# A two-layer recurrent and mixture-of-experts kernel: first layer in another order, block transposes in another bank, products added in twos on GpSimd

## The chip, the cores and the metric

The kernel runs on one core of a Trainium2 chip. The metric is the device time of one execution in microseconds (us), lower is better. A run of the kernel here means one execution; the median of three is given, and beside it one execution that the hardware profiler recorded.

## What is computed

Tokens are 8 sequences of 256, 128 features each. There are two layers. Each adds to x the product of a selective scan (a Mamba block) and a gate that is the SiLU of a mixture of eight experts. In the first layer the mixture is a hard choice of one expert for each token; in the second all eight experts work on all tokens.

```python
x = L0_attn_x
xn = _layernorm(x, axis=-1)
s = _L0_attn_ref(xn, ...)          # scan with 16 states per feature
g = _silu(_L0_ffn_ref(xn, ...))    # each token goes to its best expert of 8
x = x + s * g
xn = _layernorm(x, axis=-1)
s = _L1_attn_ref(xn, ...)          # 256 inner features, 16 states, 4 heads
g = _silu(_L1_ffn_ref(xn, ...))    # all 8 experts, weighted
x = x + s * g

# inside the scan of the first layer
def step(h, inp):
    a, bx = inp
    h = a * h + bx
    return (h, h)
y = jnp.einsum('lbdn,bln->bld', hs, C_p)

# inside the experts of the first layer: LayerNorm again, then
h = jax.nn.relu(jnp.einsum('te,td,edf->tf', onehot, xn, W1) + b1[idx])
y = jnp.einsum('te,tf,efd->td', onehot, h, W2) + b2[idx]
y = y * gates
```

## The kernel before

The program is written by hand for each engine: every engine has its own instruction list, and semaphores tie the lists together. The 2048 tokens are handled in 4 pairs of sequences (512 tokens, `T`), and a tile is 128 partitions by 512 columns.

**Slots.** Every engine walks through the same numbered slots, 32 a pair, so the first layer has slots 0 to 127, and tables of numbers say what an engine issues in which slot. A slot has no time of its own: an engine does what its list says and waits only at semaphores. In slot s, `now(TABLE, s)` gives what is due. `CH0` is the table of the scan: state g (64 in all, 16 a pair) has slot 2g in pairs 0 to 2, and every one and a half slots in pair 3.

**One state of the scan.** ScalarE forms the decay (`decay0`, L1380), VectorE multiplies the drive (`drive0`, L799) and runs the scan over 512 columns (`scan0`, L807), GpSimd multiplies the states by C (`multiply0`, L1137), and TensorE adds the product into a PSUM bank by a product with the identity (`sum_product`, L1672, three slots behind, `SUM_LAG0`). There are four state tiles (`RING`) and three product tiles (`RING_Y`): VectorE may be four states ahead of GpSimd, GpSimd three products ahead of TensorE. The rows of B and C for a state come by DMA, broadcast to 128 partitions (`load_cb0`, L495, on SyncE's queue), six states ahead.

**The routed experts.** In slots 2 to 17 GpSimd scatters the 2048 normalised tokens by expert to DRAM (`scatter`, L1074, 16 indirect DMAs). The sorted tokens then make 15 blocks of 256, each of one expert. Block b has the slot 22 + 4b (`BLOCK_AT`):
- `load_block` (SyncE, L524) loads 256 tokens, three slots before; `load_pack` (GpSimd, L1081) gathers the expert's weights into one of two buffers, four slots before, and waits there until TensorE is done with block b - 2 (`blk_down`);
- `turn_block` (TensorE, L1555) transposes the tokens into `bank[OUT_BANK]`, columns 256 to 511; it waits until ScalarE has taken out the last block's result, which is in the same bank (`blk_out_ready`);
- `turn_in` (ScalarE, L1389) in the same slot copies it out, `up_block` (TensorE, L1567) one slot later, `relu` (ScalarE, L1397) two, `down_block` (TensorE, L1575 and the bias by L1576 with one row) three, `take_out` (ScalarE, L1403) four, `store_block` (SyncE, L529) six slots later.

**Other work of the first layer.** The heads of the next pair (`head0`, tables `PE0`, `ACT0`, `DVE0`, `POOL0`) form its projections, the convolution and the softplus; the tails (`tail`) finish a pair: y, LayerNorm, output product. `split_high`/`split_low` (L1256, L658) split eight gate matrices of the second layer into a high and a low part, loaded by `load_gate` (SyncE, L475). The first of these loads waits for `fold_conv` on GpSimd (L1145, L1147), which multiplies the convolution's taps into a weight and stands between slots 31 and 32 of GpSimd's list. From slot 86 GpSimd gathers each pair's expert outputs back (`fetch`, L1092), ScalarE takes the tanh (`tanh0`, L1410), VectorE gates (`gate0`, L850, and `gated0`, L857) and GpSimd adds x (L1169).

**The start.** Statistics and two LayerNorms of all four pairs (`first_stats`, `first_norm`, `second_stats`, `second_norm`): VectorE has the sums and applies mean and root (L676), GpSimd has the root (L1058). Then come the router's logits (TensorE, L1527), the choice and the slots of the tokens (`route_choice`, `route_slots`).

**The second layer**, from 330.6 us on, has loops of its own that the change doesn't touch, but for line numbers.

## Time and profile before

| | us |
|---|---|
| median of 3 runs | 807.91 |
| lowest and highest | 806.89, 808.41 |
| the profiled execution's own time | 802.77 |
| its span, first to last instruction | 800.9 |

The profiled execution is 5.1 us below the median; 1.9 us of it lie outside the span. Over the span TensorE (PE) is busy 80%, VectorE (DVE) 71%, GpSimd (POOL) 64%, ScalarE (ACT) 56%. These shares mix two layers with different limits. In the 40 slices of the page PE has 8 or 9 tenths in nearly every slice from the 18th on, the second layer, but between 0 and 9 in the slices before it. The chain that ended last covers only 21 us at the very end, so what holds the first layer has to be read from its waits and from the timeline of each engine.

### The profile page before, as it was taken

The page shows a single profiled execution, that of the slowest core. Times are in us where ns is not written, and L with a number is a line of the kernel's source. Part 1 is how long each engine was busy: PE and PEld are TensorE (multiplying, and loading weights), DVE is VectorE, ACT ScalarE, POOL GpSimd, SP SyncE. Part 2 cuts the span into 40 slices and gives each one's busy share as a digit, 9 for nine tenths or more (in the row PEclk, how much of TensorE's full clock was granted, in tenths as well). Part 3 has the DMA queues.
Part 4 walks back from the last instruction along what each step waited for, and adds up shares of the span by engine and source line. Part 5 has one row for each costly group of instructions (what it writes and reads, how often), then busy time and mean ns, then how long its engine had stood idle before and what let it go on. Part 6 is the DMA issues. An engine that isn't in the chain of part 4 may idle for free. (4 is left out here: it accounts for less than half of the span.)

```text
span 800.9 us, 8060 instructions
## 1 busy us (share of the span) xinstructions
PE 637.1 (80%) x1974; PEld 335.7 (42%) x1974; DVE 571.3 (71%) x921; ACT 450.4 (56%) x692; POOL 511.6 (64%) x419
## 2 busy tenths in 40 slices
PE   3545758989854587589998798998889998989995
PEld 2311446656631142344443454444445444444442
DVE  8688407646754984688676877775888775889983
ACT  2432425655463155885568584568665568675650
POOL 3268535424446763488786686786578786599983
PEclk9557779979985789799999999999999999999999
DMA  8277756798765871678476377677368576388860
GB/s 241 44 220 169 226 160 214 254 305 232 222 197 164 240 191 39 177 196 213 129 197 173 105 190 174 148 184 173 108 175 201 146 176 181 108 223 212 211 171 13
DMA packets 95791, 142.24 MB, mean 178 GB/s; under 512 B 8352, under 2 KB 37088, under 8 KB 95744
## 3 DMA queue, kind: packets, MB, share of 16 engines
q1 hardware_dynamic: 92560, 130.74, 61.6%
q0 software_dynamic: 3184, 10.98, 4.0%
q8 instruction: 16, 0.26, 0.1%
q14 instruction: 31, 0.25, 0.1%
HBM read 133.23 MB, written 8.45 MB: 177 GB/s over the span
## 5 line engine op out<-in xcount | busy, mean ns | idle before, releaser
L821 DVE TENSOR_TENSOR_SCAN state<-decay,bank 128x512 f32<-128x512 f32 x128 | 155.8, 1217 | 8.6 <-issue 0.9
L1742 PE MATMUL bank<-xw,wu 128*128 128x512 f32 x256 | 138.2, 622 | 27.9 <-DVE hid L935 27.4
L1123 POOL TENSOR_TENSOR product<-state,CB 128x512 f32<-128x512 f32 x96 | 122.9, 1281 | 53.1 <-DVE state L821 50.7
L935 DVE TENSOR_TENSOR hid<-sg,bank 128x512 f32<-128x512 f32 x128 | 85.9, 671 | 67.6 <-PE bank L1742 64.2
L1752 PE MATMUL bank<-hid,wd 128*128 128x512 f32 x256 | 133.3, 603 | 0.0
L1435 ACT ACTIVATE sg<-bank 128x512 f32<-128x512 f32 x128 | 75.2, 597 | 101.9 <-PE bank L1653 92.2
L1125 POOL TENSOR_TENSOR product<-product 128x512 f32<-128x512 f32 x96 | 124.3, 1294 | 7.5
L1672 PE MATMUL bank<-product,early 128*128 128x512 f32 x128 | 81.2, 734 | 50.9 <-POOL product L1137 50.9
L814 DVE TENSOR_TENSOR bank<-bank,CB 128x512 f32<-128x512 f32 x128 | 88.7, 693 | 12.8 <-DMA CB<-crow 11.5
L1742 PEld LDWEIGHTS bank<-xw,wu 128*128 128x128 f32 x256 | 43.7, 191 | 109.3 <-issue 60.5
L1137 POOL TENSOR_TENSOR product<-state,CB 128x512 f32<-128x512 f32 x44 | 56.0, 1280 | 50.4 <-DVE state L807 50.0
L1372 ACT ACTIVATE decay<-delta,negA 128x510 f32<-128x510 f32 x128 | 82.1, 709 | 2.6 <-DVE delta L787 2.2
L807 DVE TENSOR_TENSOR_SCAN state<-decay,bank 128x512 f32<-128x512 f32 x64 | 77.9, 1217 | 7.3 <-ACT decay L1380 3.8
L1651 PE MATMUL bank<-XH,wh 128*128 128x512 f32 x128 | 75.1, 587 | 8.4 <-ACT sg L1435 7.4
L1752 PEld LDWEIGHTS bank<-hid,wd 128*128 128x128 f32 x256 | 48.6, 193 | 37.3 <-issue 30.5
L1119 POOL TENSOR_TENSOR product<-state,CB 128x512 f32<-128x512 f32 x32 | 40.8, 1276 | 34.7 <-PE bank L1664 18.1
L1672 PEld LDWEIGHTS bank<-product,early 128*128 128x128 f32 x128 | 25.2, 225 | 78.4 <-POOL product L1137 54.7
L1653 PE MATMUL bank<-XH,wl 128*128 128x512 f32 x128 | 52.7, 412 | 0.0
L1081 POOL DMA_INDIRECT wd<-pack_dram,rows_of x15 | 14.8, 986 | 59.4 <-PE bank L1576 58.9
L1652 PE MATMUL bank<-XL,wh 128*128 128x512 f32 x128 | 52.6, 411 | 0.0
L1182 POOL TENSOR_TENSOR xw<-XR,cwb 128x512 f32<-128x512 f32 x32 | 42.1, 1316 | 9.9 <-DMA cwb<-cwrow 4.4
L1380 ACT ACTIVATE decay<-delta,negA 128x510 f32<-128x510 f32 x64 | 43.7, 709 | 2.2 <-DVE delta L787 2.2
(200 smaller groups left out, 1039.0 us busy)
## 6 DMA issues: line engine op xcount, KB each, us to landing
CB<-crow SPq DMA_DIRECT2D x256, 256.0 KB, 5.0
CB<-crow SPq DMA_DIRECT2D x44, 512.0 KB, 5.9
cwb<-cwrow SPq DMA_DIRECT2D x32, 256.0 KB, 5.6
szm<-crow SPq DMA_DIRECT2D x11, 512.0 KB, 5.3
cwb<-crow SPq DMA_DIRECT2D x9, 512.0 KB, 6.3
xw<-Wg_dram SPq DMA_DIRECT2D x8, 256.0 KB, 6.6
wu<-Wu_dram SPq DMA_DIRECT2D x8, 256.0 KB, 7.1
wd<-Wd_dram SPq DMA_DIRECT2D x8, 256.0 KB, 6.8
```

The lines of the kernel that those rows point to most:

```text
L807: v.tensor_tensor_scan(state[:, g % RING, :], place0(g), drive, 0.0, ALU.mult, ALU.add).then_inc(state_ready.sem, 1)
L814: v.tensor_tensor(drive, dx, CB[:, c % ROWS, 1, :], ALU.mult).then_inc(drive_ready.sem, 1)
L821: v.tensor_tensor_scan(state[:, c % RING, :], decay[:, PLACE[c], :], drive, 0.0, ALU.mult, ALU.add).then_inc(state_ready.sem, 1)
L935: v.tensor_tensor(hid[:, u % 2, :], sg[:, PLACE[u], :], bank[UP_BANK][:, :], ALU.mult).then_inc(hid_ready.sem, 1)
L1123: p.tensor_tensor(addend, state[:, c % RING, :], cs, ALU.mult).then_inc(state_used.sem, 1)
L1125: ins = p.tensor_tensor(product[:, e % PRODS, :], product[:, e % PRODS, :], addend, ALU.add)
L1372: a.activation(by_batch(decay[:, PLACE[c], :])[:, :, 1:], by_batch(delta[:, m, :])[:, :, 1:], ACT.Exp, scale=negA[:, c:c + 1]).then_inc(de ...
L1435: a.activation(sg[:, PLACE[u], :], bank[stream_bank(u)][:, :], ACT.Silu).then_inc(silu_ready.sem, 1)
L1651: t.matmul(dst, wh[:, e, ws], XH[:, :], start=True, stop=False)
L1672: t.matmul(bank[Y_BANK][:, :], ident[:, :], product[:, g % RING_Y, :], start=(c == 0), stop=(c == N - 1)).then_inc(summed.sem, 1)
L1742: t.matmul(bank[UP_BANK][:, :], wu[:, e, 128 * f:128 * f + 128], xw[:, e % 2, :], start=True, stop=True).then_inc(up_ps.sem, 1)
L1752: ins = t.matmul(bank[OUT_BANK][:, :], wd[:, u, :], hid[:, u % 2, :], start=(u == 0), stop=(u == UNITS - 1))
```

## The change

- **Order.** The single `BLOCK_AT` becomes tables by step. With `UP_AT` = 22 + 4b, the transpose is two slots before, its copy one before, relu one after, the down product three after, the result is taken out four after: no two steps of a block that hand over to each other stand in the same slot. Pack loads stand six slots before, block loads five before. The scatters start at slot 0. The heads' slots move forward, the splits are 8 slots apart instead of 6 with three slots between high and low, and tanh and gates have later slots.
- **Banks.** The block's transpose goes to `bank[HID_BANK]`, columns 0 to 255, where the up product writes afterwards; it waits for the first two relus of the block before, no longer for its result to be taken out.
- **Packs.** Three weight buffers (`PACKS`) instead of two. The columns of x move to other tiles for it.
- **Fold first.** `fold_conv` stands before GpSimd's slots.
- **Products in twos.** `GROUP` = 2: GpSimd adds two products (32 more additions of 128x512), and TensorE adds 32 sums instead of 64, through two product tiles and an addend; `sum_group` stands four slots behind the second.
- **Start.** The LayerNorms are applied by ScalarE (`shifted`, 32 activations of 128x128); VectorE forms only the negated mean times the root (8 small operations of 128x4). One of the four logits products stands before, one behind the dt and row products, and the wait for `late_in` behind all of them.
- **Small.** The bias row of the down product becomes a full 128-row product with a matrix whose first row is one (`top_row`). ScalarE's decays run four states ahead instead of two. A wait of the expert weights' loads on a pair's y falls away, and these loads start four slots later.

```diff
-RING_Y = 3
+GROUP = 2
-PE0 = {3: "xin", 12: "z", 16: "dt", 18: "row"}
-ACT0 = {4: "xin", 11: "th", 17: "dt", 19: "row", 23: "ln"}
-DVE0 = {6: "tap1", 7: "tap2", 8: "tap3", 12: "xs", 14: "zx", 20: "rest", 26: "delta"}
-POOL0 = {21: "less"}
+PE0 = {1: "xin", 9: "z", 13: "dt", 15: "row"}
+ACT0 = {2: "xin", 8: "th", 14: "dt", 16: "row", 19: "ln"}
+DVE0 = {4: "tap1", 5: "tap2", 6: "tap3", 9: "xs", 11: "zx", 17: "rest", 21: "delta"}
+POOL0 = {18: "less"}
...
-SUM_LAG0, SUM_LAG1 = 3, 4
+SUM_LAG0, SUM_LAG1 = 4, 4
...
-SCATTER_AT = [2 + k for k in range(NT)]
-BLOCK_AT = [22 + 4 * b for b in range(BLOCKS)]
-SPLIT_AT = [34 + 6 * e for e in range(E)]
-GATHER_AT = [86, 91, 96, 111]
-TANH_AT = [89, 94, 99, 114]
-GATE_AT = [90, 95, 109, 116]
+SCATTER_AT = list(range(NT))
+UP_AT = [22 + 4 * b for b in range(BLOCKS)]
+TURN_AT, TURN_IN_AT = [at - 2 for at in UP_AT], [at - 1 for at in UP_AT]
+RELU_AT, DOWN_AT, TAKE_AT = ([at + lag for at in UP_AT] for lag in (1, 3, 4))
+PACK_AT, LOAD_AT, STORE_AT = ([at + lag for at in UP_AT] for lag in (-6, -5, 6))
+PACKS = 3
+SPLIT_AT = [30 + 8 * e for e in range(E)]
+SPLIT_LOW_AT = [at + 3 for at in SPLIT_AT]
+GATHER_AT = [86, 91, 95, 112]
+TANH_AT = [91, 95, 99, 116]
+GATE_AT = [92, 96, 109, 118]
+AHEAD = 4
...
@@ first_norm, second_norm of VectorE
-                normalise(x_rows[:, q, :, :], x_rows[:, q, :, :], mv1[:, q, :, :], rstd1[:, q, :], xn_ready)
+                negated_mean(shift1, mv1, rstd1, rstd1_ready, q, shift1_ready)
...
@@ load_pack of GpSimd
-                if b >= 2:
-                    pool.wait_ge(blk_down.sem, blk_down.at0(0, b - 1))
+                if b >= PACKS:
+                    pool.wait_ge(blk_down.sem, blk_down.at0(0, b - PACKS + 1))
...
@@ multiply0 of GpSimd
-                if g >= RING_Y:
-                    pool.wait_ge(summed.sem, summed.at0(0, g - RING_Y + 1))
-                p.tensor_tensor(product[:, g % RING_Y, :], state[:, g % RING, :], cb_pair(g)[:, 0, :], ALU.mult).then_inc(state_used.sem, 1)
+                q = g // GROUP
+                cs = cb_pair(g)[:, 0, :]
+                if g % GROUP == 0:
+                    if q >= PRODS:
+                        pool.wait_ge(summed.sem, summed.at0(0, q - PRODS + 1))
+                    p.tensor_tensor(product[:, q % PRODS, :], state[:, g % RING, :], cs, ALU.mult).then_inc(state_used.sem, 1)
+                else:
+                    pool.wait_ge(group_ready.sem, group_ready.at0(0, q))
+                    p.tensor_tensor(addend, state[:, g % RING, :], cs, ALU.mult).then_inc(state_used.sem, 1)
+                    pool.wait_ge(state_used.sem, state_used.at0(0, g + 1))
+                    ins = p.tensor_tensor(product[:, q % PRODS, :], product[:, q % PRODS, :], addend, ALU.add)
...
@@ GpSimd, after the roots
+            fold_conv()
             head0("less", 0)
-            for s in range(UNITS):
-                slot0(s)
-            fold_conv()
-            for s in range(UNITS, PAIRS * UNITS):
+            for s in range(PAIRS * UNITS):
                 slot0(s)
...
@@ turn_block of TensorE
+                if b == 0:
+                    pe.wait_ge(xnT_read.sem, xnT_read.at0(0, PAIRS))
                 if b >= 1:
-                    pe.wait_ge(blk_out_ready.sem, blk_out_ready.at0(0, b))
-                if b == 0:
-                    pe.wait_ge(lg0_ready.sem, lg0_ready.at0(0, 1))
+                    pe.wait_ge(blk_relu.sem, blk_relu.at0(0, FT * (b - 1) + 2))
                 for k in range(2):
-                    last = t.transpose(bank[OUT_BANK][:, BLOCK + 128 * k:BLOCK + 128 * k + 128], blk_x[:, b % 2, k, :], ident[:, :])
+                    last = t.transpose(bank[HID_BANK][:, 128 * k:128 * k + 128], blk_x[:, b % 2, k, :], ident[:, :])
...
@@ down_block of TensorE
-                    last = t.matmul(dst, ones128[0:1, :], pack[0:1, b % 2, PACK_COLS - D:PACK_COLS], start=False, stop=True)
+                    last = t.matmul(dst, top_row[:, :], pack[:, b % PACKS, PACK_COLS - D:PACK_COLS], start=False, stop=True)
```

How it moves instructions. TensorE's queue, one block in the middle of the blocks, before: the names are `hid` (tokens of a block, to be transposed), `product` (a state's product, to be added), `sg` (the transposed tokens, then the relu's result), `wd` (the pack of weights).

```order
L1555 MATMUL bank<-early,hid 128x128 x2
L1672 MATMUL bank<-product,early 128x512
L1567 MATMUL bank<-sg,wd 128x256 x4
L1672 MATMUL bank<-product,early 128x512
L1575 MATMUL bank<-wd,sg 128x128 x4
L1576 MATMUL bank<-wd,ones 128x128
L1575 MATMUL bank<-wd,sg 128x128 x4
L1576 MATMUL bank<-wd,ones 128x128
```

The same place now:

```order
L1721 MATMUL bank<-product,early 128x512
L1611 MATMUL bank<-sg,wd 128x256 x4
L1601 MATMUL bank<-early,hid 128x128 x2
L1623 MATMUL bank<-wd,sg 128x128 x4
L1624 MATMUL bank<-wd,top_row 128x128
L1623 MATMUL bank<-wd,sg 128x128 x4
L1624 MATMUL bank<-wd,top_row 128x128
```

The transpose of the next block has moved from behind the down product to between the up and the down product of this block, and one of the two sums is gone.

GpSimd's queue while it scatters (`wu` holds the normalised tokens, `CB` the rows of C), before:

```order
L1137 TENSOR_TENSOR product<-state,CB 128x512
L1074 DMA sorted_in<-wu,slot_of 3840x128 x2
L1137 TENSOR_TENSOR product<-state,CB 128x512
L1074 DMA sorted_in<-wu,slot_of 3840x128 x2
L1137 TENSOR_TENSOR product<-state,CB 128x512
```

and now:

```order
L1154 TENSOR_TENSOR product<-state,CB 128x512
L1087 DMA sorted_in<-wu,slot_of 3840x128 x2
L1158 TENSOR_TENSOR product<-state,CB 128x512
L1160 TENSOR_TENSOR product<-product 128x512
L1087 DMA sorted_in<-wu,slot_of 3840x128 x2
```

An addition stands in the queue for every four scatters; the first scatter stands ahead of the first product.

## Rows read from the trace of the kernel before

**Rows 1.** Windows by stage: PE, PEld, DVE, ACT, POOL busy; PEclk, DMA share, GB/s.

```profile
43.50:85.80 42.30, 21.33 (x29) 6.31 (x29) 31.74 (x35) 10.64 (x17) 35.13 (x32) 0.66 0.71 187
85.80:232.00 146.20, 124.24 (x564) 85.22 (x564) 84.36 (x120) 79.34 (x155) 59.85 (x52) 0.92 0.73 225
232.00:330.60 98.60, 50.09 (x118) 20.84 (x118) 60.82 (x115) 44.64 (x74) 52.24 (x46) 0.76 0.64 176
330.60:800.90 470.30, 423.55 (x1204) 211.71 (x1204) 362.27 (x494) 299.84 (x422) 353.80 (x277) 0.98 0.64 164
```

**Rows 2.** Waits, 85.8 to 232 us: who for whom, total us, times, longest.

```profile
POOL wd L1081 <- PE bank L1576: 58.9, 13, 11.2
...
PE bank L1555 <- DMA hid<-sorted_in: 11.4, 2, 8.5
```

**Rows 3.** Waits of SyncE's DMA queue, 0 to 330 us, same columns.

```profile
SPq L475 <- POOL later L1147: 18.1, 1, 18.1
```

**Rows 4.** Timeline of GpSimd: start, us, instruction; the convolution's fold.

```profile
105.82 2.08 POOL L1145 TENSOR_TENSOR w_cv<-w_cv,later 128x256 f32<-128x256 f32 x3
```

**Rows 5.** Timeline of TensorE, one undisturbed block; counts are passes, two a product.

```profile
156.09 0.38 PE L1555 MATMUL bank<-early,hid 128*128 128x128 f32 x2
156.30 1.02 PE L1672 MATMUL bank<-product,early 128*128 128x512 f32 x2
157.16 1.95 PE L1567 MATMUL bank<-sg,wd 128*128 128x256 f32 x8
158.95 1.02 PE L1672 MATMUL bank<-product,early 128*128 128x512 f32 x2
160.05 1.16 PE L1575 MATMUL bank<-wd,sg 128*128 128x128 f32 x8
161.13 0.48 PE L1576 MATMUL bank<-wd,ones 1*128 1x128 f32 x2
...
163.68 0.41 PE L1555 MATMUL bank<-early,hid 128*128 128x128 f32 x2 [0.56 <-ACT hid L1403]
```

**Rows 6.** Timeline of ScalarE: the four relus of that block.

```profile
158.35 1.64 ACT L1397 ACTIVATE sg<-bank,wd 128x256 f32<-128x256 f32 x4 [0.19 <-PE bank L1567]
```

**Rows 7.** Timeline of GpSimd while it scatters.

```profile
59.77 0.95 POOL L1074 DMA_INDIRECT sorted_in<-wu,slot_of  x1 [0.30 <-issue]
...
63.49 0.96 POOL L1074 DMA_INDIRECT sorted_in<-wu,slot_of  x1 [0.30 <-issue]
...
77.17 1.01 POOL L1074 DMA_INDIRECT sorted_in<-wu,slot_of  x1 [0.17 <-issue]
```

**Rows 8.** The page's costliest groups: the second layer's additions on GpSimd.

```profile
L1125 POOL TENSOR_TENSOR product<-product 128x512 f32<-128x512 f32 x96 | 124.3, 1294 | 7.5
```

**Rows 9.** Timeline of TensorE: the first block's transpose.

```profile
85.77 0.69 PE L1555 MATMUL bank<-early,hid 128*128 128x128 f32 x2 [2.88 <-DMA hid<-sorted_in]
```

**Rows 10.** Timelines of SyncE, GpSimd, ScalarE and VectorE: last block's store to second gate.

```profile
231.83 0.47 SPq L529 DMA_DIRECT2D sorted_out<-hid  x1
...
238.13 1.00 POOL L1092 DMA_INDIRECT sg<-sorted_out,slot_of  x1 [6.47 <-DMA sorted_out<-hid]
...
244.45 1.27 ACT L1410 ACTIVATE yfT<-sg,hp 128x128 f32<-128x128 f32 x4 [9.23 <-DMA sg<-sorted_out,slot_of]
...
258.52 1.34 DVE L850 SCALAR_TENSOR_TENSOR yfT<-yfT,sg 128x512 f32<-128x512 f32 x1 [4.53 <-ACT yfT L1410]
```

**Rows 11.** Timeline of VectorE: last scan of the first layer, first step of the second.

```profile
310.68 1.22 DVE L807 TENSOR_TENSOR_SCAN state<-decay,bank 128x512 f32<-128x512 f32 x1
...
330.63 0.69 DVE L793 TENSOR_TENSOR bank<-delta,xs 128x512 f32<-128x512 f32 x1
```

**Rows 12.** Timeline of VectorE: the router's logits.

```profile
34.61 0.29 DVE L702 TENSOR_TENSOR sz<-bank,brb 128x128 f32<-128x128 f32 x1 [6.85 <-PE bank L1527]
```

**Rows 13.** One line's durations in ns, min/median/max: the convolution's taps on VectorE.

```profile
L748 DVE SCALAR_TENSOR_TENSOR sp_e<-xpad,early,sp_e x12: 726/745/1793, 14.7 to 207.5; 128x512 f32<-128x512 f32 x12
```

**Rows 14.** Timeline of TensorE: a down product after a wait.

```profile
170.27 1.98 PE L1575 MATMUL bank<-wd,sg 128*128 128x128 f32 x8 [2.67 <-ACT sg L1397]
```

156 lines of the change are left out of this document (94 added, 62 removed).

## The prediction, made before the changed kernel had run

> **What bounds the kernel now.** I read the windows by stage first [rows 1]. The second layer, from 330.6 us on, has TensorE (PE) busy 423.6 of 470.3 us at a granted clock of 0.98, and no line of it is changed: it stays at 470.3 us. The first layer takes 330.6 us, and in none of its stages is one engine full, but for the 146.2 us of the expert blocks, where PE is busy 124 us. So the question is what the engines wait for there. The waits of that stage [rows 2] name GpSimd's pack loads first: 58.9 us in 13 times, each for the end of a down product of PE. GpSimd's queue is in order, so behind that wait stand the products, behind them VectorE's scans (four state tiles) and PE's own sums. Next is PE's wait for a block of tokens, 11.4 us in two pieces. SyncE's own waits say where it comes from [rows 3]: it stood 18.1 us at the first gate matrix's load, which waits for the convolution's fold on GpSimd, and the next block's load is queued behind. The fold ran at 105.8 us [rows 4], because GpSimd itself sat in a pack load's wait.
>
> PE's timeline shows the floor below these stalls: an undisturbed block goes from transpose to transpose in 163.68 - 156.09 = 7.59 us [rows 5]. The stage took, from the first transpose at 85.77 [rows 9] to the last store at 231.83 [rows 10], 146.1 us for 15 blocks, 9.74 each.
>
> **Start: earlier, but it doesn't reach the end.** VectorE waited 6.85 us for the logits, to 34.61 [rows 12]; the LayerNorms leave its queue and the heads' products move ahead of the last logits. The slot loop began at 43.5 (where the first window of [rows 1] begins) and can come at most those 6.85 us sooner, and at worst no sooner; since the choice and the slots of the tokens hang on these logits and nothing else is late, I take 4.8, to 38.7. But then GpSimd sets the pace until the scatters are out. Two slots cost it 63.49 - 59.77 = 3.72 us (two scatters, one product) [rows 7]. Now four slots also hold an addition, 1.29 us [rows 8] and 0.06 of issue: 2 x 3.72 + 1.35 = 8.8 us. The first scatter goes at about 37.7, slot 3 ends at about 49.4, twelve more slots take 3 x 8.8 = 26.4, so the last scatter ends at about 76.2 instead of 77.17 + 1.01 = 78.2 [rows 7]. The chain from there to the first transpose was 85.77 - 78.18 = 7.6 us and stays: **-1.9 us** (-4.0 and +2.9 at the ends of the start's range). The moved slots of the heads are hidden here: PE is busy half of that stage, ScalarE a quarter [rows 1].
>
> **Block stage: -27 us.** A third pack buffer puts GpSimd's wait at the down product of block b - 3, nine slots behind the up product for which the pack comes, and the load stands six before it: three slots of slack where there was one. Fold first removes SyncE's 18.1 us. So PE's own cycle is left. Its parts by starts [rows 5]: sum 0.86; up product 1.79; down product (160.05 to 163.12, less the wait) 3.0; transpose 0.25. One sum goes. The transpose doesn't wait 0.56 for the result's removal any more. The bias product of one row takes 0.42 (161.13 to 161.55), a full one 0.27 (an eighth of 1.16 for a pass, two passes): -0.15 twice. That leaves 0.86 + 1.79 + 2.7 and a gap: relus end 1.64 after their start, which came 158.35 - 157.16 = 1.19 after the up product's [rows 6], so down starts 2.9 after up, and in between stand 1.79 of up and the next block's transpose. Sum: 0.86 + 2.9 + 2.7 = 6.5 us. In this gap the four heads of a pair are hidden; the tails (y, yn, s) partly.
>
> Other engines in four slots: busy time of the stage over its 15 blocks [rows 1] is 84.4 / 15 = 5.6 us on VectorE, 79.3 / 15 = 5.3 on ScalarE and 59.9 / 15 + 1.35 = 5.3 on GpSimd. All are below PE, but VectorE has more than its mean in the first half of a pair, where heads and tails stand and its tail and PE's wait for each other in turn, and ScalarE's logarithm with its table loads once let PE wait 2.67 us [rows 14]. DMA moved 225 GB/s at a share of 0.73 [rows 1]: the same bytes in 117 us want a share of 0.9, so landings will be late at times. Between 6.5 and the old 9.7 I take 7.7, near the undisturbed 7.59, since what goes (1.7 us) is in part eaten by the first half of the pair and by DMA. 15 x 7.7 = 115.5, and 2 for the low clock of the first block and 1.5 from last down to store: 119 against 146.1.
>
> A rule of the Trainium skill speaks on one term: "TensorE: Matmul & The Clock Gate", section "Why this matters for your kernels", says that a product with 32 rows takes as long as one with 128. By it the full bias row would give nothing, and the block 0.3 us more, 4.5 us over the stage. The trace shows the one-row product at 0.42 against 0.27, and the measurement goes first.
>
> **Gathers: -1.5 us.** The second gate came 258.52 - 231.83 = 26.7 us after the last store [rows 10]. In the new order: the store lands after 238.13 - 231.83 = 6.3, and GpSimd has three products and two additions of 1.3 ahead of the second fetch, 6.5. The gathers are 4 x (0.95 + 0.30), as the scatters cost [rows 7]; the tanh began 244.45 - 238.13 - 4.8 = 1.5 behind them and takes 1.3 [rows 10]: store + 6.3 + 4.8 + 6.5 + 4.8 + 1.5 + 1.3 = 25.2. A store that lands sooner, since the expert weights load later now, would give up to 3 more. GpSimd is full here, where before it waited for VectorE.
>
> **Pair 3 and the end: -2 us.** From the second gate to the end of the last scan VectorE needed 311.9 - 258.5 = 53.4 us, to the second layer's first step 18.7 more, a chain of heads through PE, ScalarE and VectorE [rows 11]. GpSimd now has 16 products, 8 additions, four gathers, three small roots and residuals in it: 31.6 + 4.8 + 5 = 41, below 53. So VectorE still leads. The last gate now stands behind the softmax of the next layer's head instead of ahead of it; so its wait for the last gathers leaves the chain. No row prices that; between 0 and -4 I take 2.
>
> **Sum.** -1.9 - 27 - 1.5 - 2 = -32.4: the span 800.9 becomes 768.5. The profiled execution lay 5.1 us below the median of 807.91; I take the difference from the median: **775.5 us**.
>
> **The rivals.**
> - *PE's cycle is reached.* The engines interlock without loss and a block takes 7.0: 105 + 3.5 = 108.5 in the stage, 10.5 us less; with 3 more in the gathers 762. For it: the heads fit into the gap. Against: VectorE's load in the first halves and DMA at a share near 1.
> - *DMA is next.* Packs and blocks land late and a block takes 8.5: 131 us, -15 instead of -27, 787.5. For it: the undisturbed block above ran while DMA had 0.89, and the whole stage already had 0.73 [rows 1]. Against: packs are asked for six slots ahead, some 11 us.
> - *The additions are on the path.* GpSimd gets 32 x 1.35 = 43 us. Eight lie among the scatters and are counted; if the eleven from slot 84 on all show (15 us), less the 2.6 counted in the gathers, it is 788. For it: GpSimd has the gathers there. Against: 52 of 98.6 us busy [rows 1].
> - *Two inputs, one port.* The Trainium skill ("SBUF — State Buffer", section "Who interferes with whom") says that a VectorE operation with two inputs in SBUF and a GpSimd operation that reads SBUF exclude each other. The taps show something like it: 745 ns in the middle, 1793 at most [rows 13]. Scan and drive read one of their inputs from PSUM. Some 10 operations a pair could each wait up to 1.05, 40 us if all did; the taps' median says that few do, and I count 3 us, within the forecast's range.
> - *Slower: PE falls to the low clock.* Granted clock in the block stage was 0.92. After a wait of 2.67 us the same eight passes took 1.98 instead of 1.16 us [rows 5, 14]. With one sum less PE has a gap of 0.9 us in every block. If the clock fell to 1.2 GHz for the whole stage, PE's 5.4 us would be 9.3 and the block about 11: 165 + 3.5 against 146.1, +22.4 instead of -27, 825. It decides from some 65% of the blocks at the low clock; below that the change still wins. Against: at 156 to 164 us PE kept 0.6 us idle a block at the full clock.
> - *The change does not do what it says:* if turn, up and relu still wait in turn, a block takes 7.6 to 8.5, which lies in the cases above, as GpSimd's and SyncE's long waits go in any case.
>
> **How the numbers follow.** Forecast 0.60 (766 to 784), PE's cycle reached 0.14, DMA 0.11, additions 0.10, low clock 0.04, anything near no change 0.01. A measurement of this kernel can tell about 0.2% from no change, 1.6 us. Faster: 0.95; same: 0.01; slower: 0.04. The range holds the forecast and reaches to the first three rivals: 757 to 792.
>
> **What would show it.** In the profile after: the first transpose at about 84 us; the last block's store near 203; GpSimd's waits at the pack loads near nothing, SyncE's at the first gate matrix gone; transposes 7 to 8 us apart; the second layer's first step near 298 and 470 us behind it. If transposes are 8.5 apart with PE waiting for DMA, the second rival holds; if VectorE waits for GpSimd after slot 84, the third; a clock well below 0.9 in the block stage, the slow one. I am wrong if the second layer's 470 us change or if the scatter stage gives back more than the start gains.

## The result, and the profile after

The changed kernel takes **784.9 us** (median of 4 runs, 779.8 to 786.0) where the kernel before takes 808.2 beside it: a ratio of **0.969**, 95% interval 0.964 to 0.975. It is faster by 23 us where the prediction had 32. The profiled execution took 784.66 us (span 782.8); that of before 802.77, which was 5 us under its own median, so between the two traces there are 18.1 us to be found. Three executions further below, one each of e6, e7 and e8, took over 1.5% longer than the fastest of their kernel; the ratios leave them out, the medians don't, and that of e6 is the one of its trace.

The windows by stage of the changed kernel, cut at its first block transpose, its last store, its second gate and the first step of the second layer (columns as in [rows 1]: busy time of PE, PEld, DVE, ACT, POOL; then granted clock, DMA share, GB/s):

```profile
42.50:82.40 39.90, 13.37 (x14) 3.92 (x14) 25.06 (x27) 12.57 (x18) 35.63 (x32) 0.89 0.65 165
82.40:208.45 126.05, 102.93 (x530) 80.14 (x530) 84.61 (x120) 72.84 (x149) 82.74 (x67) 0.89 0.84 259
208.45:237.92 29.47, 5.28 (x6) 1.30 (x6) 17.60 (x20) 9.58 (x20) 21.69 (x19) 0.59 0.70 200
237.92:309.56 71.64, 41.06 (x94) 16.46 (x94) 50.11 (x99) 35.94 (x56) 47.66 (x41) 0.67 0.62 172
309.56:782.80 473.24, 426.29 (x1204) 212.83 (x1204) 362.96 (x494) 300.02 (x422) 353.82 (x277) 0.97 0.65 163
```

Read against [rows 1] and [rows 9 to 11], the block stage gained by far the most, 146.1 to 126.0 us. The start gained 3.4 (first transpose at 82.4 instead of 85.8). The way from the last store to the second gate got longer, 26.7 to 29.5; from there to the end of the last scan shorter, 53.4 to 49.3; from there to the second layer longer, 18.7 to 22.3; and the second layer, whose code is the same, took 473.2 instead of 470.3. The sum is -3.4 - 20.0 + 2.8 - 4.1 + 3.6 + 3.0 = -18.1.

The waits of the block stage (who waited for whom, total us, times, longest):

```profile
POOL wd L1094 <- PE bank L1624: 11.2, 6, 4.2
...
PE bank L1601 <- DMA hid<-sorted_in: 13.2, 3, 4.7
...
PE bank L1556 <- DVE wu L684: 7.5, 2, 3.7
...
DVE wu L684 <- POOL rstd_t L1071: 5.8, 2, 2.9
```

GpSimd's 58.9 us of waits for pack buffers [rows 2] are 11.2, and SyncE's 18.1 us at the first gate matrix [rows 3] are gone. TensorE's waits for tokens are not: 13.2 us in three pieces, of which 4.7 are the first block's. In the kernel before they were 11.4 in two pieces, and one of them, 2.9 us, was the first block's too ([rows 2], [rows 9]). Behind the first block TensorE waited 8.5 us before and waits 8.5 us now: once for block 2 then, twice for 4.1 and 4.4 us now. One late block is cured, and two others are late now.

An undisturbed block, on TensorE's timeline (start, us, instruction; a product of 32-bit floats is two passes):

```profile
100.32 0.41 PE L1601 MATMUL bank<-early,hid 128*128 128x128 f32 x2 [0.16 <-ACT sg L1435]
101.09 1.16 PE L1623 MATMUL bank<-wd,sg 128*128 128x128 f32 x8 [0.36 <-ACT sg L1435]
102.09 0.39 PE L1624 MATMUL bank<-wd,top_row 128*128 128x128 f32 x2
102.31 1.06 PE L1623 MATMUL bank<-wd,sg 128*128 128x128 f32 x8
...
103.43 1.02 PE L1721 MATMUL bank<-product,early 128*128 128x512 f32 x2
104.29 1.89 PE L1611 MATMUL bank<-sg,wd 128*128 128x256 f32 x8
106.40 0.41 PE L1601 MATMUL bank<-early,hid 128*128 128x128 f32 x2 [0.22 <-ACT sg L1435]
```

It takes 6.08 us from transpose to transpose where it took 7.59 [rows 5]. The stage took 8.4 a block all the same, some 30 us in all above such blocks. Two kinds of place account for a good half of this (18 us, by e7 below). First, tokens that come late; second, the root of the LayerNorm on GpSimd. Both stand in the timelines of SyncE, PE, GpSimd and VectorE:

```profile
82.66 1.78 SPq L533 DMA_DIRECT2D hid<-sorted_in  x1
...
92.36 0.69 PE L1601 MATMUL bank<-early,hid 128*128 128x128 f32 x2 [4.08 <-DMA hid<-sorted_in]
92.85 1.92 PE L1623 MATMUL bank<-wd,sg 128*128 128x128 f32 x8
...
118.65 1.27 POOL L1158 TENSOR_TENSOR product<-state,CB 128x512 f32<-128x512 f32 x1 [2.87 <-DVE state L818]
120.00 1.26 POOL L1160 TENSOR_TENSOR product<-product 128x512 f32<-128x512 f32 x1
121.22 1.04 POOL L1071 TENSOR_TENSOR rstd_t<-veps_t,half 128x4 f32<-128x4 f32 x1
...
122.30 1.36 DVE L684 TENSOR_SCALAR wu<-bank,mv_t,rstd_t 128x128 f32<-128x128 f32 x4 [2.90 <-POOL rstd_t L1071]
...
123.72 1.12 PE L1556 MATMUL bank<-early,wu 128*128 128x128 f32 x4 [3.73 <-DVE wu L684]
```

Block 1's tokens were asked for at 82.66 and let TensorE start at 92.36; the eight passes behind that wait took 1.92 us instead of 1.06, at the lower of the two clocks (granted clock 0.50 from 92.3 to 94.8 us). At 118 to 124 us the small root waits in GpSimd's queue behind a product and its addition, VectorE waits 2.90 us for the root and TensorE 3.73 us for VectorE. The same happens one pair later. The addition is the change's own: in the kernel before, the root stood behind a product alone, and VectorE waited for it once, 1.8 us.

From the last store to the second gate (SyncE, GpSimd, ScalarE, VectorE), to be read beside [rows 10]:

```profile
208.45 0.47 SPq L538 DMA_DIRECT2D sorted_out<-hid  x1
...
216.11 1.00 POOL L1105 DMA_INDIRECT sg<-sorted_out,slot_of  x1 [5.52 <-DMA sorted_out<-hid]
...
227.88 0.99 POOL L1105 DMA_INDIRECT sg<-sorted_out,slot_of  x1
...
236.61 1.28 ACT L1448 ACTIVATE yfT<-sg,hp 128x128 f32<-128x128 f32 x4 [11.72 <-DMA sg<-sorted_out,slot_of]
...
237.92 0.82 DVE L861 SCALAR_TENSOR_TENSOR yfT<-yfT,sg 128x512 f32<-128x512 f32 x1 [4.86 <-ACT yfT L1448]
```

The store took 7.7 us to land instead of 6.3; the second fetch came 11.8 us behind the first, as counted (11.3); but ScalarE began 8.7 us behind the start of the second fetch, where 4.8 + 1.5 = 6.3 had been counted.

The last head (ScalarE, PE, VectorE), to be read beside [rows 11]:

```profile
286.62 1.28 ACT L1314 ACT_TABLE_LOAD   x1
...
291.17 1.10 PE L1561 MATMUL bank<-xs,later 128*96 128x512 f32 x2 [3.38 <-ACT sz L1369]
292.95 2.08 PE L1677 MATMUL bank<-XNP,later 128*128 128x512 f32 x2 [0.68 <-ACT rows L1377]
...
296.66 2.07 PE L1561 MATMUL bank<-rows,w_dt 32*128 32x512 f32 x2
```

The head's exponential needs a table load of 1.28 us here. In the kernel before, the scans' last decays, exponentials too, stood close ahead of this head and had brought the table off the chain; now the last decays are done sooner, another function has been loaded since, and the load lies in the chain. TensorE's wait for the same product grows from 1.10 to 3.38 us, and behind it two products take 2.08 and 2.07 us instead of 1.12 and a sum 1.91 instead of 1.02, at a granted clock of 0.58 from 291.0 to 298.7 us. The load and the slower products make 4.1 us; since this head also began 0.6 us sooner against the last scan's end, 3.6 are lost. This is read from the traces; no run tried another order on ScalarE. The Trainium skill ("ScalarE: Activation LUTs", section "What ACT_TABLE_LOAD costs") gives 1283 ns for a load and 2.66 us with a drain for a switch. The trace agrees on the load; it shows the next activation 1.29 us behind the load's start and the load right behind the activation ahead of it, so no drain beside it.

### The profile page after: what moved, and what is told of

The parts are those of the page before. It is cut to its first block and busy times, and to the rows that moved or that the text cites. A ratio compares the mean times of both kernels' runs of the same rounds, so it can differ in the third digit from the quotient of the medians.

```text
span 782.8 us, 7991 instructions
## 1 busy us (share of the span) xinstructions
PE 609.7 (78%) x1910; PEld 328.3 (42%) x1910; DVE 567.7 (73%) x899; ACT 461.5 (59%) x724; POOL 555.9 (71%) x451
## 5 line engine op out<-in xcount | busy, mean ns | idle before, releaser
L1792 PE MATMUL bank<-xw,wu 128*128 128x512 f32 x256 | 140.0, 629 | 28.1 <-DVE hid L946 27.8
L1136 POOL TENSOR_TENSOR product<-state,CB 128x512 f32<-128x512 f32 x96 | 122.9, 1280 | 54.7 <-DVE state L832 52.2
L1473 ACT ACTIVATE sg<-bank 128x512 f32<-128x512 f32 x128 | 75.3, 597 | 102.7 <-PE bank L1701 91.2
L946 DVE TENSOR_TENSOR hid<-sg,bank 128x512 f32<-128x512 f32 x128 | 85.9, 671 | 67.7 <-PE bank L1792 64.2
L1138 POOL TENSOR_TENSOR product<-product 128x512 f32<-128x512 f32 x96 | 124.2, 1294 | 7.5
L1721 PE MATMUL bank<-product,early 128*128 128x512 f32 x64 | 46.9, 824 | 59.7 <-POOL product L1160 59.7
L1699 PE MATMUL bank<-XH,wh 128*128 128x512 f32 x128 | 75.7, 591 | 8.4 <-ACT sg L1473 7.4
L1132 POOL TENSOR_TENSOR product<-state,CB 128x512 f32<-128x512 f32 x32 | 40.8, 1276 | 37.2 <-DVE state L832 19.6
L1721 PEld LDWEIGHTS bank<-product,early 128*128 128x128 f32 x64 | 13.1, 251 | 76.7 <-POOL product L1160 58.3
L1160 POOL TENSOR_TENSOR product<-product 128x512 f32<-128x512 f32 x32 | 41.5, 1298 | 2.5
L1410 ACT ACT_TABLE_LOAD x32 | 41.1, 1283 | 0.6
```

Of the source, the lines that this page charges most:

```text
L946: v.tensor_tensor(hid[:, u % 2, :], sg[:, PLACE[u], :], bank[UP_BANK][:, :], ALU.mult).then_inc(hid_ready.sem, 1)
L1136: p.tensor_tensor(addend, state[:, c % RING, :], cs, ALU.mult).then_inc(state_used.sem, 1)
L1138: ins = p.tensor_tensor(product[:, e % PRODS, :], product[:, e % PRODS, :], addend, ALU.add)
L1410: a.activation(by_batch(decay[:, PLACE[c], :])[:, :, 1:], by_batch(delta[:, m, :])[:, :, 1:], ACT.Exp, scale=negA[:, c:c + 1]).then_inc(de ...
L1473: a.activation(sg[:, PLACE[u], :], bank[stream_bank(u)][:, :], ACT.Silu).then_inc(silu_ready.sem, 1)
L1699: t.matmul(dst, wh[:, e, ws], XH[:, :], start=True, stop=False)
```

## The experiments

All runs are compared with the kernel before on the same chip, by ratio and 95% interval; the stages are read from each run's trace, at the same five cuts as above. The table has the numbers on which the verdicts rest (us). The runs come in four groups, in which the kernel before took 808.2 (changed), 810.6 (again, e1 to e3), 805.4 (e4 to e6, v1) and 809.3 us (v1 again, e7, v2, e8): medians compare within such a group, ratios across them. Each row has one trace, so a stage's time is that of one execution.

| kernel | median | ratio (95%) | first transpose | blocks | store to gate | to last scan | to layer 2 | layer 2 |
|---|---|---|---|---|---|---|---|---|
| before | 808.2 | 1 | 85.8 | 146.1 | 26.7 | 53.4 | 18.7 | 470.3 |
| changed | 784.9 | 0.969 (0.964-0.975) | 82.4 | 126.0 | 29.5 | 49.3 | 22.3 | 473.2 |
| changed, again | 785.2 | 0.969 (0.964-0.974) | 82.9 | 126.5 | 28.9 | 49.5 | 21.0 | 476.3 |
| e1 tokens 8 ahead | 779.6 | 0.963 (0.958-0.968) | 81.8 | 119.0 | 28.7 | 50.5 | 23.9 | 474.6 |
| e2 root sooner | 777.8 | 0.961 (0.956-0.966) | 82.3 | 118.1 | 28.1 | 51.7 | 22.5 | 473.9 |
| e3 no additions | 775.7 | 0.958 (0.953-0.963) | 78.2 | 122.4 | 27.4 | 49.3 | 22.0 | 473.8 |
| e4 before + fold first | 797.6 | 0.990 (0.983-0.997) | 86.8 | 136.6 | 26.8 | 53.4 | 18.7 | 470.2 |
| e5 before + third pack | 800.3 | 0.990 (0.982-0.997) | 86.2 | 139.8 | 26.8 | 53.4 | 21.1 | 472.3 |
| e6 before + both | 792.1 | 0.979 (0.971-0.987) | 85.9 | 135.6 | 26.6 | 53.6 | 18.7 | 477.3 |
| v1 = e1 + e2 + e3 | 766.3 | 0.948 (0.942-0.955) | 75.9 | 114.5 | 28.1 | 50.3 | 21.2 | 475.2 |
| v1 again | 764.7 | 0.944 (0.941-0.948) | 76.0 | 116.4 | 28.7 | 49.6 | 21.6 | 473.6 |
| e7 = e1 + e2 | 766.6 | 0.949 (0.945-0.954) | 81.9 | 107.8 | 28.7 | 51.8 | 21.2 | 467.3 |
| v2 added in blocks only | 762.5 | 0.940 (0.935-0.944) | 75.3 | 113.1 | 25.8 | 49.4 | 21.8 | 477.7 |
| e8 = v1 + one-row bias | 769.4 | 0.950 (0.946-0.955) | 76.3 | 118.5 | 27.9 | 49.2 | 22.0 | 473.1 |

The theory: the change gained by the order and the waits it took away, and lost some 9 us of that to late tokens and to a root behind an addition. The main rival: the additions themselves are too dear, wherever they stand.

**The changed kernel again**, no edit.

> The changed kernel once more, unaltered, as the measure for the runs beside it. Expected 785 us (780 to 788), a ratio to the kernel before of 0.970 (0.964 to 0.975). It also asks which waits of the first trace are the program's and which are chance. The waits of the block stage that the order fixes (3.7 us twice for yn, the late token blocks 1 and 8 at about 4 us each, the 17 us of VectorE for wh) should come again within 1 us; the dip of the granted clock to 0.76 at 375 to 380 us in the second layer, which the kernel before didn't have behind the same 1.3 us wait, should be gone if it was chance, and the second layer then takes 470 us again instead of 473.2.

The time came again. The waits for yn came within 1 us. VectorE's for `wh` did not (13.2 us instead of 17.6), nor did the tokens': behind the first block TensorE waited 13.4 us in four times instead of 8.5 in two, and block 1's transpose came at 95.8 instead of 92.4. So a late block is the program's, how late is chance. The second layer did not go back to 470 (476.3).

**e1: tokens eight slots ahead.**

```diff
-PACK_AT, LOAD_AT, STORE_AT = ([at + lag for at in UP_AT] for lag in (-6, -5, 6))
+PACK_AT, LOAD_AT, STORE_AT = ([at + lag for at in UP_AT] for lag in (-6, -8, 6))
```

> One edit of the changed kernel: the block of tokens is asked for eight slots ahead of its up product instead of five. Theory (late blocks): TensorE's two waits for a block, 4.1 and 4.4 us, with the passes at 1.2 GHz behind them (about 1.5 and 2), go or shrink below 1 us; the first layer loses 6 to 10 us, ratio 0.958 to 0.963. Rival (the transfers themselves are the limit, share 0.84 in the stage): the earlier block only pushes pack loads back, TensorE waits for packs or other blocks instead, and the time stays within 2 us (0.967 to 0.972). Rival 3: the load now stands ahead of a store or of the gate matrices in SyncE's queue and waits for its buffer to come free, so that the stage gets longer by some us.

The theory holds: -5.6 us, and 7.0 to 7.5 in the block stage, some of it given back behind it. TensorE's timeline at blocks 1 and 2:

```profile
87.97 0.42 PE L1601 MATMUL bank<-early,hid 128*128 128x128 f32 x2 [0.16 <-DMA hid<-sorted_in]
97.00 0.44 PE L1601 MATMUL bank<-early,hid 128*128 128x128 f32 x2 [0.76 <-DMA hid<-sorted_in]
```

Block 1 starts 4.4 us sooner than in the changed kernel. The transfers were late because they were asked for late. Behind the first block TensorE waits for tokens more than 1 us only once, 1.9 us.

**e2: the root one slot sooner.**

```diff
-POOL_TAIL = {39: "yn2"}
+POOL_TAIL = {38: "yn2"}
```

> One edit of the changed kernel: GpSimd's small root of yn stands one slot earlier in its queue, ahead of the product and the addition of the slot (2.6 us) that it stood behind. Theory (root behind the addition): VectorE's waits for the root, 2.90 us each at 122.3 and 187.3, fall below 1, TensorE's two waits of 3.7 us for yn fall to about 1, and the low clock at 124 to 128 goes; 4 to 7 us off the stage, ratio 0.961 to 0.966. Rival (VectorE was late itself, and the root only came last): the root now waits for VectorE's sums instead, GpSimd's product and addition behind it come later, and the time stays within 1.5 us.

The theory holds: -7.4 us, at the better end of the expected ratio, and 7.9 to 8.4 in the block stage, a little more than expected. VectorE and PE, at the place that is shown above for the changed kernel:

```profile
121.32 1.36 DVE L684 TENSOR_SCALAR wu<-bank,mv_t,rstd_t 128x128 f32<-128x128 f32 x4
...
122.73 0.66 PE L1556 MATMUL bank<-early,wu 128*128 128x128 f32 x4 [0.74 <-DVE wu L684]
```

VectorE doesn't wait, TensorE waits 0.74 us instead of 3.73 and keeps its clock (four transposes in 0.66 us instead of 1.12).

**e3: no additions.** Each product goes to TensorE as it is, 64 sums instead of 32, through three product tiles; a sum stands three slots behind its product instead of four. The main lines:

```diff
-                    ins = p.tensor_tensor(product[:, q % PRODS, :], product[:, q % PRODS, :], addend, ALU.add)
...
+                if g >= 3:
+                    pool.wait_ge(summed.sem, summed.at0(0, g - 3 + 1))
+                p.tensor_tensor(product[:, g % 3, :], state[:, g % RING, :], cb_pair(g)[:, 0, :], ALU.mult).then_inc(state_used.sem, 1)
```

> The changed kernel without the additions: each state product goes to TensorE as it is, 64 sums more for TensorE in the first layer and none of GpSimd's 32 additions. Its order, third pack buffer, fold and bias product stay. Theory (the additions give TensorE a sum a block and cost GpSimd 1.3 us for it; the two nearly cancel): the scatter stage is shorter by 5 x 1.35 = 4 to 7 us, the block 0.9 us of TensorE longer (a cycle of about 6.9 instead of 6.1) but with no wait for the root, the gathers 2.6 us shorter: together within 5 us either way, ratio 0.964 to 0.974. If the additions carry the gain of the block stage, 15 x 0.9 = 13 us go and the ratio is 0.984. If they stand on the path behind slot 84, as one rival of the prediction has it, it is 8 to 12 us faster, 0.956.

It is 9.5 us faster than the changed kernel. That is the price of the last case, but not its place. Against the changed kernel run beside it, 4.7 us lie ahead of the first transpose, 4.1 in the block stage and 1.5 at the gathers. GpSimd's scatters, four slots apart:

```profile
48.64 1.03 POOL L1087 DMA_INDIRECT sorted_in<-wu,slot_of  x1 [0.30 <-issue]
...
56.30 0.96 POOL L1087 DMA_INDIRECT sorted_in<-wu,slot_of  x1 [0.30 <-issue]
```

Four slots take 7.66 us, and 9.07 in the changed kernel. In the block stage undisturbed transposes are 5.9 to 7.2 us apart instead of 6.0 to 6.4: there an addition does spare TensorE something, and the kernel with additions loses it again at its waits, the two for the root among them.

**e4, e5, e6: parts of the change in the kernel before.** e4 puts the fold ahead of head "less" and of the first slot; e5 makes three pack buffers, for which the columns of x move to other tiles; e6 does both.

```diff
+            fold_conv()
             head0("less", 0)
-            for s in range(UNITS):
-                slot0(s)
-            fold_conv()
-            for s in range(UNITS, PAIRS * UNITS):
+            for s in range(PAIRS * UNITS):
                 slot0(s)
```

The third buffer (main lines):

```diff
-                if b >= 2:
-                    pool.wait_ge(blk_down.sem, blk_down.at0(0, b - 1))
-                p.indirect_dma_start(pack[:, b % 2, :], None, w["pack"], bass.IndirectOffsetOnAxis(rows_of[:, b:b + 1], 0)).then_inc(pack_in[b % 2].sem, 16)
+                if b >= 3:
+                    pool.wait_ge(blk_down.sem, blk_down.at0(0, b - 2))
+                p.indirect_dma_start(pack[:, b % 3, :], None, w["pack"], bass.IndirectOffsetOnAxis(rows_of[:, b:b + 1], 0)).then_inc(pack_in[b % 3].sem, 16)
```

> The kernel before with one edit: the convolution's fold stands first in GpSimd's and ScalarE's order, ahead of the scatters' slots, as in the changed kernel. Theory: SyncE's 18.1 us at the first gate matrix's load goes, block 2's tokens come in time, and TensorE loses most of its 11.4 us of waits for tokens; but GpSimd's 58.9 us of waits for pack buffers stay, and a part of what TensorE gains turns into waits for packs: block stage -4 to -8 of 146, ratio 0.990 to 0.995. Rival (pack buffers alone hold the stage): the same time within 0.3%. Rival 2 (the fold's matrix work delays the scatters by its 1 to 2 us): slower by 0.2%.

> The kernel before with one edit: three pack buffers in place of two; order, sums and bias product stay. Theory: GpSimd's 58.9 us of waits for down products fall below 15; the fold and with it SyncE's gate matrix come sooner by themselves, as GpSimd was late with the fold for a pack's sake; block stage -10 to -14 of 146, ratio 0.982 to 0.988. Rival (GpSimd's waits were slack, and TensorE's order of sum, transpose, up, relu, down sets 9.7 us a block): -3 us or less, ratio above 0.996.

> The kernel before with both edits, fold first and three pack buffers: all that the change does to waits for buffers and loads, and nothing of its order, additions and bias product. Theory: the block comes down to the undisturbed 7.6 us of the kernel before plus late transfers, a stage of about 128 (-18 of 146), ratio 0.978 (0.972 to 0.984). The changed order is then worth the 8 to 10 us from there to the changed kernel without its additions (ratio 0.958 in the run before). Rival (the order carries the gain): -8 us or less here, ratio above 0.989.

e4 and e5 are each 1% faster than the kernel before, with intervals from 0.3 to 1.8%. The waits of the block stage of e4:

```profile
POOL wd L1081 <- PE bank L1574: 52.1, 13, 9.5
```

and of e5:

```profile
POOL product L1138 <- DVE state L808: 72.8, 23, 11.3
...
POOL wd L1082 <- PE bank L1577: 2.2, 2, 1.6
```

e4 left 52 of the 58.9 us of GpSimd's waits where they were and still took 9.4 us off the stage, more than the 4 to 8 expected; e5 took away all but 2.2 of them and gained 6.3, about half of what was expected. GpSimd then waited 72.8 us for VectorE's states instead, where it had waited 26.7: the largest wait of the profile was mostly slack. In the traces both edits together gave 10.5 us of the stage, not the 15.7 of their sum. A reason is at hand: each also cures part of what the other does, since SyncE's 18.1 us at the gate matrix are 9.8 in e5 already. The expected 18 was too much by 7.5: where nothing was late, the old order's transposes stayed 7.6 to 9.0 us apart. The whole times don't show the overlap, though. e4 and e5 have 0.990 each, and e6 has 0.979, which is what the two make together and what was expected (0.978). With intervals of 0.8% to either side this decides nothing, and how far the two gains overlap stays open.

So by the traces about 10.5 of the 20 us of the block stage belong to fold and buffers. The step from there to the kernel without additions (135.6 to 122.4, 13.1 us) is everything else: the new order and banks, the full bias product (2 to 4 us by e8), the moved heads and splits, the decays further ahead. The additions as placed took 3.6 back. Order alone was not run, so its share is a difference and not a measurement.

**v1: the three gains together.**

> The changed kernel without the additions, with the block of tokens asked for eight slots ahead and GpSimd's root of yn one slot sooner: the three edits that each gained, together. Theory (they remove different waits): without the additions TensorE still waited 9.3 us for tokens; 6 of them go. The root then waited for no addition, so it gives 1 to 2 at most. Expected 769 us (765 to 773), ratio 0.951 (0.945 to 0.956). Rival (their gains are the same microseconds, since a freer GpSimd already let the loads come sooner): 774 to 776, ratio 0.957 as without the additions alone.

It came at the fast end of what was expected: 766.3 us, 0.948, and 764.7, 0.944, in a second set of runs, whose expectation was

> The version without additions, with the two earlier placements, once more, as the measure for the three runs beside it: a ratio of 0.948 (0.943 to 0.953), a block stage of 114.5 us with pure blocks at 5.9 to 6.0.

**e7: both placements, additions kept.** The two diffs of e1 and e2.

> The changed kernel with its additions kept and the two earlier placements (tokens eight slots ahead, root of yn one slot sooner). The two placements alone gave 7.1 and 8.2 us in the block stage of the changed kernel, 126. Theory (they remove different waits, and the additions then cost what they cost in the first scatters and the gathers, but give TensorE a sum a block): T0 stays at 82, block stage 112 (110 to 116), total 771 (768 to 775), ratio 0.953 (0.949 to 0.958), 4 to 5 us above the version without additions. Rival (the additions cost nothing once the placements are mended): ratio 0.948, as without them. Rival 2 (GpSimd is full in the block stage): 118 there, ratio 0.960.

The windows of its block stage and its second layer:

```profile
81.89:189.66 107.77, 94.59 (x530) 71.66 (x530) 88.94 (x121) 73.32 (x149) 83.75 (x68) 0.97 0.94 309
...
291.31:758.60 467.29, 422.27 (x1204) 210.85 (x1204) 362.38 (x494) 299.90 (x422) 353.67 (x277) 0.98 0.67 165
```

The block stage was expected at 112 us and took 107.8, the shortest of all, with the DMA engines at a share of 0.94 and 309 GB/s: the transfers had not been the limit at 0.84. v1's stage is 6.7 to 8.6 longer, and its first transpose 5.9 sooner. The medians are 1.9 us apart, and the intervals overlap. In total e7 is at 0.949, which is the first rival's number and not the theory's 0.953. So once tokens and root are in time the additions cost 1.9 us, within the noise of nothing, where they cost the changed kernel 9.5: that was mostly the price of their place, and the rival (they are too dear wherever they stand) has no support. By the traces they gain in the block stage what they cost in the scatters, but the size of that gain is uncertain, for e7's trace is its fastest execution (760.4 us, its median 766.6) and v1's second one its slowest (767.8, median 764.7).

**v2: additions only in the block stage.** Products of slots 16 to 79 are added in twos, the others go one by one; the placements are those of v1. The main lines:

```diff
+TWOS = range(4, 20)
+SUMS0 = [u for q in range(PAIRS * N // 2) for u in ([(2 * q, 2 * q + 1)] if q in TWOS else [(2 * q,), (2 * q + 1,)])]
...
+                for n, gs in enumerate(SUMS0):
+                    if s == CH0[gs[-1]] + (4 if len(gs) == 2 else 3):
+                        sum_mixed(n)
```

> The version without additions and with the two earlier placements, but with the 16 additions of the groups from slot 16 to 79 put back: products are added in twos only where the expert blocks run, and go to TensorE one by one in the scatter and gather stages. Theory (an addition buys TensorE time only where TensorE is full, which is the block stage: 104.8 of 114.5 us busy there): the first block's transpose stays at 76, the block stage gets 0.86 a block shorter where nothing else holds it, 114.5 becomes 106 to 110, and the rest stays: 760 us (757 to 764), ratio 0.941. Rival (DMA, at a share of 0.88 in that stage, or VectorE is next at once): 113 to 115 in the stage, ratio 0.947. Rival 2 (GpSimd's longer queue delays the scans there): slower, 0.951.

```profile
75.30:188.38 113.08, 97.70 (x533) 73.71 (x534) 90.14 (x122) 76.73 (x155) 83.38 (x67) 0.95 0.90 297
...
285.35:763.00 477.65, 431.63 (x1204) 214.84 (x1204) 362.71 (x494) 300.17 (x422) 353.81 (x277) 0.96 0.66 162
```

762.5 us is the best median, 6% below the kernel before and 3% below the changed one. It doesn't prove its reason. The stage took 113.1 us in the trace, not 106 to 110. Late tokens are not why: behind the first block TensorE waited 3.3 us for them, and 2.4 in v1's second trace. The last block shows another reason (ScalarE, GpSimd, SyncE):

```profile
183.24 0.38 ACT L1443 ACTIVATE hid<-bank 128x256 f32<-128x256 f32 x1 [0.91 <-PE bank L1626]
...
184.23 1.27 POOL L1160 TENSOR_TENSOR product<-state,cwb 128x512 f32<-128x512 f32 x1 [5.56 <-PE bank L1725]
...
188.38 0.47 SPq L545 DMA_DIRECT2D sorted_out<-hid  x1
```

The first single product behind the pairs, slot 80, goes to the tile of the last pair (`TILE0`), so GpSimd waits 5.56 us for TensorE's sum of that pair. SyncE's loads of the rows of B and C wait for GpSimd (4.6 us), and the last store stands behind them: it goes 4.8 us after its result was taken out, in e7 1.1 us after. These 3.6 us are the edit's own, at the place where pairs end; without them the stage would be 109.5 us, an estimate from the two traces that no run tried. A part is given back behind the store (25.8 us to the gate, v1 28.1 and 28.7). And the intervals of v1 (0.941 to 0.948) and v2 (0.935 to 0.944) overlap. That the two placements and this one together beat the changed kernel is certain; that v2 beats v1 is not.

**e8: the one-row bias product in v1.**

```diff
-                    last = t.matmul(dst, top_row[:, :], pack[:, b % PACKS, PACK_COLS - D:PACK_COLS], start=False, stop=True)
+                    last = t.matmul(dst, ones128[0:1, :], pack[0:1, b % PACKS, PACK_COLS - D:PACK_COLS], start=False, stop=True)
```

> The version without additions and with the two earlier placements, with the bias product of one row put back in place of the full one of 128 rows (two per block, 30 in all). It was sized in the prediction at 0.15 us a product, 4.5 us over the stage; the changed kernel's trace shows starts 0.22 apart where it was 0.42. Theory: down products take 0.4 us longer a block; where TensorE is full (9 or 10 of 15 blocks) this shows, pure blocks at 6.3 instead of 5.9, stage +4 to +6, ratio 0.953. Rival (a product with one row takes as long as a full one, as the Trainium skill, page TensorE: Matmul & The Clock Gate, section Why this matters for your kernels, says of 32 rows): no change, 0.948. Rival 2 (DMA or another engine sets the block in any case): the product is longer but the stage the same within 1.5 us.

TensorE's timeline in e8:

```profile
106.80 1.05 PE L1609 MATMUL bank<-wd,sg 128*128 128x128 f32 x8
107.78 0.48 PE L1610 MATMUL bank<-wd,ones 1*128 1x128 f32 x2
108.20 1.16 PE L1609 MATMUL bank<-wd,sg 128*128 128x128 f32 x8
...
109.70 1.99 PE L1597 MATMUL bank<-sg,wd 128*128 128x256 f32 x8
```

and the same block in v1 (second run):

```profile
107.08 1.05 PE L1609 MATMUL bank<-wd,sg 128*128 128x128 f32 x8
107.97 0.39 PE L1610 MATMUL bank<-wd,top_row 128*128 128x128 f32 x2
108.20 1.06 PE L1609 MATMUL bank<-wd,sg 128*128 128x128 f32 x8
...
109.31 1.89 PE L1597 MATMUL bank<-sg,wd 128*128 128x256 f32 x8
```

From the first down pass to the up product it is 2.90 us with one row and 2.23 with 128, and the up product's passes begin 0.1 slower too: undisturbed blocks are 6.67 to 6.73 us apart instead of 5.9. The stage grew by 2.1 to 4.0 us and the median by 4.6; the intervals (0.946 to 0.955, 0.941 to 0.948) overlap a little, so the product's time is shown and that of the whole kernel is likely. The first theory holds in kind; a block lost twice what was expected (0.77 us, not 0.4), and the stage less than the blocks, since TensorE's short waits took up the rest.

## Why the prediction held, and where it was wrong

The range (757 to 792) held the 784.9, and the sign was right. The forecast's own range (766 to 784) was missed by 0.9 us: with 23 us of 32, the result lies between the forecast and the two rivals at 788.

- **Start, -1.9 us: measured -3.4.** The scatters' time was right (9.07 us for four slots, 8.8 counted; last scatter at 75.7 + 1.0, 76.2 counted). The chain behind them was 5.7 us instead of 7.6: the step "7.6 us and stays" was the one off. Only four of the additions lie among the scatters, as the sum of this term has it, and not the eight of the third rival.
- **Block stage, -27 us: measured -20.0.** This is the term that was missed, in two directions. TensorE's cycle was sized at 6.5 us and is 6.1: the down product takes 2.34 (101.09 to 103.43) where 2.7 was counted, since the bias product gave 0.77 a block in all (e8) and 0.3 was counted. What the stage lays on top was sized at 7.7 - 6.5 = 1.2 us a block and is (126.0 - 3.5) / 15 - 6.1 = 2.1. The prediction priced heads and tails as VectorE's load and asked for packs; it put the wait for tokens down to the fold whole (11.4 us in two pieces), though 2.9 of it were the first block's and untouched by it; and it looked neither at how many slots ahead the tokens are asked for (e1: 7 us) nor at what the addition pushes back in GpSimd's own queue, the root (e2: 8 us). With both placed well the stage is 107.8, below the forecast of 119.
- **What fold and packs are worth** was not priced apart, but the text named GpSimd's 58.9 us of waits first. e5 shows that their size misled: with all but 2.2 us of them gone, the stage gained 6.3 us and the kernel 1%.
- **The low clock** was counted with 2 us for the first block. It came behind the long waits instead; the granted clock of the stage was 0.89 and is 0.97 in e7, where most of the waits are gone.
- **Gathers, -1.5 us: measured +2.8.** The additions (2.6) were counted and there. The store landed 1.4 us later, and the tanh came 2.4 us later behind the fetches than counted. While the second fetch ran, expert weights were loaded by SyncE; whether that is the cause was not tried.
- **Pair 3 and the end, -2 us: measured -4.1 and +3.6.** The first piece gave the full bound of 4. The traces fit the reason that was given (the last gate waited 2.86 us for the tanh before and doesn't wait now), but no run tried it. The chain of heads, 18.7 us and taken as unchanged, got a table load and then TensorE's low clock. The order on ScalarE was not read for its tables.
- **Second layer, 0: measured +3.0**, in the changed kernel and, in other runs, from -3.0 to +7.4 with the same code (see below). The prediction named a change of these 470 us as a sign that it is wrong. The sign came, but it is no wider than what one and the same program shows: the changed kernel took 473.2 and 476.3 us there.
- **The rivals.** *PE's cycle is reached* is what e7's trace has: 107.8 us of stage, where this rival said 108.5. *DMA is next* came near in size (a block at 8.5, measured 8.2 by the same sum) for the wrong reason: a share of 0.94 was reached in e7. *The additions are on the path* came near in size too (12 us more, 9.5 in e3), but only 1.5 us of that lay between the last store and the second gate and next to nothing behind it, where the rival had placed it. *Two inputs, one port* did not show: the taps took 745 ns in the middle and 1030 at most, the scans 1220 as before. Nor did *the low clock throughout*. The change did what it says: transposes of undisturbed blocks stand no more behind ScalarE's removal.
- **Other signs.** The last store was to come near 203 us and came at 208.4, the second layer near 298 and came at 309.6; GpSimd's waits at the pack loads were to be near nothing and are 11.2 us. A change of 0.2% was to be told from none; the interval here is 0.5% to either side.

That the forecast was missed by 9.4 us only is in part luck. Between the two traces 18.1 us were gained where 32.4 were counted, 14.3 less; by the medians it is 9.4 less, because the traced execution of the kernel before was 5 us under its median. And the errors of the stages lie on both sides: the start (1.5) and the last scans (2.1) came better than counted, the block stage (7.0), the gathers (4.3), the last heads (3.6) and the second layer (3.0) worse.

## What to carry to other kernels

A wait's size is not its price: 59 us of waiting for a buffer were worth 6 of the stage, since another engine set the pace behind it; ask what is late next before adding up. When work is added to an in-order queue, look for the small, urgent instruction behind it (a 1 us root on GpSimd cost 8) and move that ahead, and when a stage gets faster, move its loads further ahead by the same step. An addition on GpSimd that spares TensorE a product costs its full time where GpSimd sets the pace (7.66 us for four slots without it, 9.07 with it); where TensorE is full it seems to pay, and it can be chosen stage by stage, if the tiles are laid out for the place where the two kinds meet. Functions that change places on ScalarE change who pays for the table load.

## What the hardware showed that was not expected

- **A product of one row is slower than one of 128.** The next product starts 0.42 us behind the start of its two passes, against 0.22 to 0.23, and the products behind it are slower by 0.1 (2.90 us against 2.23 in the lines of e8). The Trainium skill ("TensorE: Matmul & The Clock Gate", section "Why this matters for your kernels") has a product with 32 rows at the same time as one with 128; for one row between products of 128 the runs here show otherwise. Why is open: the one-row weights' own load is no longer (182 ns against 192). What differs in the same lines is the load's start: with 128 rows it begins 0.11 us ahead of the product (107.86, the product at 107.97), with one row together with it (both at 107.78).
- **The second layer's time moves by 10 us with the same instructions**, from 467.3 (granted clock 0.98) to 477.7 (0.96), in the windows of e7 and v2 above. Busy time of VectorE, ScalarE and GpSimd is the same within 0.4 us; TensorE's moves by 9.4. One place in the changed kernel:

```profile
375.00:380.00 5.00, 4.46 (x7) 1.73 (x8) 2.83 (x4) 3.71 (x7) 4.76 (x4) 0.76 0.21 61
```

Behind a wait of 1.34 us TensorE ran at the lower clock for a part of these 5 us; behind the same wait at 396 us in the kernel before it did not. All fourteen traces have this wait. In the 5 us from 0.5 us before its end, the granted clock is 0.69 to 0.78 in eight of them and 1.00 in six, and the two traces of v1, one and the same program, have 0.73 and 1.00. So the dip is a matter of the single execution. Whether the changed order makes such dips likelier is open: four traces with the old order have 470.2 to 477.3 (one dip), ten with the new one 467.3 to 477.7 (seven).
